# Two NF4 matrices turned within an attention's last batch, and the order of the start: a four-layer kernel on one core

## What is computed

```python
x = x + _L0_xattn_ref(_layernorm(x), ctx, w_in, b_in, w_out, b_out, w_ct, b_ct, 64)
x = x + _L0_ffn_ref(_layernorm(x), weight1, weight2, weight3)
...
def _L0_xattn_ref(mask, encodings, ...):      # 16 batches, 8 heads of 16, 512 tokens
    q, k, v = split(mask^T @ w_in.T + b_in)
    scores = where(|i - j| <= 64, q k^T / 4, min)
    o = softmax(scores) v @ w_out.T + b_out
    return (relu(o^T) * encodings) through w_ct, + b_ct
...
def _L0_ffn_ref(x, weight1, weight2, weight3):
    w1, w2, w3 = nf4_roundtrip(each)          # blocks of 64, scales quantised again
    return (silu(x w1^T) * (x w2^T)) w3^T     # 1408 hidden columns
```

## Time and profile before

| | |
|---|---|
| Runs, median (lowest to highest) | 1455.07 us (1453.42 to 1456.38) |
| Profiled execution, its own time | 1452.38 us |
| Its span on the core | 1450.6 us |
| Mean granted clock of PE | 0.979 |
| Busy: PE, DVE, ACT, POOL | 93%, 67%, 54%, 17% |
| First attention, up to the barrier | 0 to 476 us |
| Turning of weights and first rows | 476 to 492.6 us |

### The profile page before, as it was taken

The page is one execution under the profiler, slowest core; times in us unless marked ns, Lnnn a source line. Parts: engine busy times, 40 slices in busy tenths (PEclk is TensorE's granted clock), DMA queues, the critical chain, the costliest instruction groups (busy, mean ns, idle before and its releaser), DMA issues. The chain is left out here.

```text
span 1450.6 us, 28759 instructions
## 1 busy us (share of the span) xinstructions
PE 1355.9 (93%) x8732; PEld 818.1 (56%) x8732; DVE 977.6 (67%) x3234; ACT 788.2 (54%) x1802; POOL 245.7 (17%) x265
## 2 busy tenths in 40 slices
PE   3688999999999899999989999998788999999998
PEld 1345656565555444444455555555434877777774
DVE  6988999999996545546456788777568655444211
ACT  4877888888878533332367666667420233333231
POOL 3100000000000100000011000013311255555452
PEclk7799999999999999999999999999999999999999
DMA  8634353434430400000020000000413588898885
GB/s 258 172 79 99 81 123 96 117 95 111 108 82 10 146 0 0 0 0 1 0 76 15 16 16 14 14 0 31 151 70 111 165 259 251 246 255 251 243 243 116
DMA packets 63186, 149.52 MB, mean 103 GB/s; under 512 B 10792, under 2 KB 27830, under 8 KB 58892
## 3 DMA queue, kind: packets, MB, share of 16 engines
q1 hardware_dynamic: 49836, 115.70, 26.4%
q0 software_dynamic: 13280, 32.93, 9.9%
HBM read 113.21 MB, written 35.39 MB: 102 GB/s over the span
## 5 line engine op out<-in xcount | busy, mean ns | idle before, releaser
L777 DVE CUSTOM_DVE_ANT_0 masked_scores<-ps_max,band_mask 128x192 bf16<-128x192 f32 (+1 forms) x512 | 176.7, 382 | 17.7 <-PE ps_max L508 12.8
L386 ACT ACTIVATE probs_t<-ps_sc 128x448 f32<-128x448 f32 x256 | 139.1, 544 | 67.8 <-PE ps_sc L528 67.7
L1256 PE MATMUL f_ps<-f_xt,w_t 128*128 (+1 forms) x704 | 160.2, 382 | 2.5 <-ACT w_t L1311 2.5
L380 ACT ACTIVATE nf_above<-nf_scaled,nf_sign_at 128x512 f16<-128x512 bf16 x231 | 161.9, 717 | 0.0
L2804 DVE TENSOR_TENSOR d_inter<-d_silu_g,d_su 128x384 f32<-128x384 f32 x32 | 17.7, 554 | 161.7 <-PE d_su L2488 156.4
L1928 ACT ACTIVATE c_probs<-d_sg,c_negmax 128x128 f32<-128x128 f32 x256 | 90.3, 365 | 58.3 <-DVE c_negmax L2013 57.9
L508 PE MATMUL ps_max<-k_stack,q_stack 96*128 96x192 bf16 (+1 forms) x512 | 95.9, 271 | 26.7 <-DMA k_stack<-dr_parts 12.7
L1256 PEld LDWEIGHTS f_ps<-f_xt,w_t 128*128 128x128 bf16 x704 | 69.3, 98 | 86.7 <-issue 4.9
L2321 POOL DMA_INDIRECT out<-d_h,d_scatter_now x64 | 97.3, 1520 | 107.2 <-DMA out<-d_h,d_scatter_now 90.4
L2672 DVE TENSOR_SCALAR d_onehot<-d_slot_no,d_pos 128x192 bf16<-128x192 bf16 x512 | 101.0, 288 | 0.3 <-PE d_lb L2389 0.3
L508 PEld LDWEIGHTS ps_max<-k_stack,q_stack 96*128 96x128 bf16 x512 | 45.7, 100 | 93.8 <-issue 64.0
(11 more groups left out here) (385 smaller groups left out, 2869.3 us busy)
## 6 DMA issues: line engine op xcount, KB each, us to landing
d_wgu<-in_ex_gu SPq DMA_DIRECT2D x32, 1024.0 KB, 6.9
d_wdown<-in_ex_d SPq DMA_DIRECT2D x32, 512.0 KB, 6.1
dr_parts<-qk_parts SPq DMA_DIRECT2D x32, 384.0 KB, 4.9
q_stack<-dr_parts SPq DMA_DIRECT2D x32, 192.0 KB, 2.8
k_stack<-dr_parts SPq DMA_DIRECT2D x32, 192.0 KB, 3.4
out<-x_sb SPq DMA_DIRECT2D x21, 256.0 KB, 2.1
nf_w<-in_nf_w POOLq DMA_DIRECT2D x3, 1408.0 KB, 9.3
q_stack<-dr_parts SPq DMA_DIRECT2D x32, 128.0 KB, 2.4
```

The source lines that it names most:

```text
L380: act.activation(above[:, g, k, :], lvl[:, g, :], ACT.Sign, bias=cut[:, k - NDV:k - NDV + 1]).then_inc(s_sg, 1)
L386: act.activation(pt[:, c, :], SP[c % 2][:].rearrange("p a w -> p (a w)")[:, a:z], ACT.Exp, scale=D0 ** -0.5).then_inc(s_e, 1)
L777: op = dve.tensor_tensor_reduce(masked[:, c % 2, k, off:off + hi - lo], M[c % 2][:, k, off:off + hi - lo], mask[:, k, off:off + hi - lo], ...
L1256: mm = pe.matmul(bank[:], w12[:, m, kt, ft * P:(ft + 1) * P], xt[:, q, kt, bass.ds(g * N, N)], start=(kt == 0 and q == 0), stop=(kt == KT ...
```

## The change

There are four edits, and a new memory layout that two of them need. In the code of the change the lines are higher by 17 to 49.

1. **ACT's start.** The second batch's parts stand ahead of all twelve row sums instead of behind four of them.
2. **First maxima.** SP writes and reads them, behind both batches' stack loads and ahead of its loop; POOL goes from the first matrix's maxima straight to the wait for the stacks and the two NF4 loads.
3. **Scales in batch 1.** `block_sums` and `block_recip` stand at step 4 instead of 5 of the first half; `block_scales` stands at step 2 instead of 3 of the second half.
4. **Turning.** The twelve banks of matrices 1 and 2 are turned by PE in batch 15 into the two `ps_max` banks (free there) and copied by DVE: bank 0 at step 2 and 1 to 3 at steps 5 to 7 of the first half, 4 to 11 at steps 0 to 7 of the second. The feed-forward phase turns the six of matrix 3, with x after four (`xs` = 4); the matmul of the hidden scale stands after four banks instead of seven.

For 4 the tile `w12_t` exists from the start. Until batch 15 it holds the q and k stacks of even batches and the scratch of the block maxima (`nf_fold`); those of odd batches are a tile of their own (`stacks_odd`), so POOL's memset of ones is two of half the size, one behind the other. Later phases put tiles of theirs into the same room.

```diff
+CH_W = FF * D // P // CH
+def w12_banks():
+    return [[(m * CH_W * CH + f * D + kt * P, m, f) for f in range(ft, min(ft + 2, FT)) for kt in range(KT)]
+            for ft in range(0, FT, 2) for m in range(2)]
...
+    EARLY_AT = [[[], [], [0], [], [], [1], [2], [3]], [[4], [5], [6], [7], [8], [9], [10], [11]]]
+    turned_bank = lambda n: M[n % 2][:].rearrange("p a w -> p (a w)").bitcast(BF16)[:, 0:len(early[n]) * P]
...
             for i in range(2):
                 write_parts(i, i)
                 for g in range(2):
                     load_stack(i, i, g, 16)
+            sp.wait_ge(s_mp, 2)
+            sp.dma_start(dr_max[0].rearrange("c a t -> a c t"), mparts[:]).then_inc(s_mw0, 16)
+            sp.wait_ge(s_mw0, 16)
+            sp.dma_start(qst[0][96:98, 0:4, :], dr_max[0].rearrange("c (h q) t -> c h (q t)", h=4)).then_inc(s_mr0, 16)
...
             pool.wait_ge(s_am, 1)
             gather_maxima(0, 1)
-            pool.wait_ge(s_mp, 2)
-            pool.dma_start(dr_max[0].rearrange("c a t -> a c t"), mparts[:]).then_inc(s_mw0, 16)
-            pool.wait_ge(s_mw0, 16)
-            pool.dma_start(qst[96:98, 0, 0:4, :], dr_max[0].rearrange("c (h q) t -> c h (q t)", h=4)).then_inc(s_mr0, 16)
             pool.wait_ge(s_ld[0], 192)
...
             root(2, DVE_ROWS)
-            for b in range(DVE_ROWS, DVE_ROWS + 4):
-                row_sum(b)
             for k in range(2):
                 first_part(1, 1, k)
             for k in range(2):
                 second_part(1, k)
-            for b in range(DVE_ROWS + 4, NB):
+            for b in range(DVE_ROWS, NB):
                 row_sum(b)
...
+            def turn_w12(n):
+                if n == 0:
+                    pe.wait_ge(s_nw, 2 * CH_W)
+                    pe.wait_ge(s_mx, 8 * 2 * NB)
+                if n == 1:
+                    pe.wait_ge(s_mp, 4 * NB)
+                if n >= 2:
+                    pe.wait_ge(s_wTc, n - 1)
+                bank = turned_bank(n)
+                for t, (col, m, f) in enumerate(early[n]):
+                    mm = pe.transpose(bank[:, t * P:(t + 1) * P], wn[:, col:col + P], identb[:])
+                mm.then_inc(s_wT, 1)
...
+                    if final:
+                        for n in EARLY_AT[0][c]:
+                            turn_w12(n)
...
+            def copy_w12(n):
+                m, f0, cnt = early[n][0][1], early[n][0][2], len(early[n])
+                dve.wait_ge(s_wT, n + 1)
+                dve.tensor_copy(w12[:, m, :, f0 * P:f0 * P + cnt // KT * P].rearrange("p k (f c) -> p f k c", c=P),
+                                turned_bank(n).rearrange("p (f k c) -> p f k c", k=KT, c=P)).then_inc(s_wTc, 1)
...
-                    if c == 5 and second:
+                    if c == 4 and second:
                         block_sums(1, 3)
                         block_recip(1, 3)
...
-                    if c == 3 and second:
+                    if c == 2 and second:
                         block_scales(1, 3)
...
         for ft in range(0, FT, 2):
-            for m in range(2):
-                out.append([(m * 5632 + f * D + kt * P, m, f) for f in range(ft, min(ft + 2, FT)) for kt in range(KT)])
-        for ft in range(0, FT, 2):
             out.append([(2 * 5632 + kt * FF + f * P, 2, f) for f in range(ft, min(ft + 2, FT)) for kt in range(KT)])
...
-    order, on_act, xs, count = [], [], 11, {"a": 0, "d": 0}
+    order, on_act, xs, count = [], [], 4, {"a": 0, "d": 0}
```

81 lines of the change are left out of this document (50 added, 31 removed).

## The result

| | before | changed |
|---|---|---|
| median of the runs shown, us | 1455.07 | 1461.52 |
| profiled execution, us | 1452.38 | 1457.74 |
| its span, us | 1450.6 | 1456.0 |
| mean granted clock of the span | 0.979 | 0.974 |

The ratio of the times is 1.0056, with a 95% interval of 1.0041 to 1.0072: slower by 8 us (6 to 10.5); the two medians of the table lie 6.45 apart, which that interval takes in. By either number the result is outside the range of the prediction, 1451.0 to 1459.0. In a later comparison the changed kernel had 1.0060 (1.0041 to 1.0078). The change makes the kernel slower, by more than 0.2%.

A forecast was written before the change was run, and what follows sets the result against it. The prediction took PE as the bound, nine tenths busy in nearly every slice, with gains only where PE waits. Its terms, 0 + 1.8 - 1.9 + 4.5 - 4.6 + 0.5, gave +0.3: 1455.4 us, range 1451.0 to 1459.0.

The forecast's parts named there:

- The four places: Where the change touches waits: the start, the second batch, the last batch, and the start of the feed-forward phase.
- term 3: Second batch: block scales one step earlier shrink DVE's 2.32 wait and gain 1.9 us, bounds 0 and -2.3.
- term 2: Start: first maxima on SP go behind the stack loads, their read lands late for PE: +1.8 us, 0 to 3.6.
- Term 5: Start of the feed-forward phase: fewer banks and copies bring the hidden products 4.6 us sooner, bounds -4 and -5.2.
- Term 6: TensorE's clock behind the feed-forward head: the 1.2 GHz stretch reaches further into hidden products, +0.5 us, bounds -1.7 and +1.7.
- signs of being wrong: Last batch grows by under 3 us, PE waits over 3 us for first maxima, or the whole start gets shorter.
- Term 1: Start: ACT's second-batch parts, moved ahead of four row sums, still wait for the first batch's write: 0.
- rival (b): Start: the first maxima's read lands beyond 47 under the NF4 loads; net +3.8 us, 1458.9; chance 0.15.
- Term 4: Last batch: turning twelve banks costs PE 88 transposes, nearly none hidden, +4.5 us, bounds 2.5 and 5.1.
- rival (a): Last batch: the turning hides beside the softmax, term 4 is 2.5 or less; about -2.9 us, 1452.2; chance 0.25.
- Rival (c): Feed-forward head: sparse work keeps PE at 1.2 GHz into the hidden products; net +2.0 us, 1457.1; chance 0.1.

The follow-up runs named there:

- fillers: Transposes of the identity that compute nothing, added to keep PE at work in the head: on the turning alone 0.9994, on nine banks 0.9986, on the kernel before 0.9999.
- the turning alone: The kernel before with only the turning of the twelve banks in the last batch, parts 1, 2 and 3 undone: 1.0023 of the kernel before.
- the memset held: The turning alone, all six remaining banks turned ahead of x's rows, POOL's memset held until DVE has written the last row's halves: 1.0009 of the kernel before.
- the two kernels with nine banks: Turning alone, rows last and memset held, but three of twelve banks back in the head: 1.0021; the same with identity transposes keeping PE at work: 0.9986.

## Why the prediction was wrong

**What bounds the kernel, and the places.** The four places were the right ones, and at each the wait named is the one that changed. The sum was +0.3 and the times show +8.1. Two terms make up most of the gap: term 3 forecast a gain of 1.9 that is not there, and term 2 was too small by 1.2 to 3.1. Terms 5 and 6 add a little each. The range was also too narrow for the terms: with every term at its bad bound (0, +3.6, 0, +5.1, -4.0, +1.7) they add up to +6.4, or 1461.5, while the range ended at 1459.0 and was said to take in the bounds of the terms. At the good end terms 2, 3 and 5 give -2.5 and not -3. One of the signs of being wrong that the prediction named came true: a wait of over 3 us for the first maxima, which was 4.32.

**Term 1 (ACT's order, 0): right.** 1.0002 (0.9988 to 1.0016) alone.

**Term 2 (first maxima on SP, +1.8, bounds 0 to 3.6): too small, and the step that failed is "I take 1.8, the middle, since the NF4 loads are only beginning".** Alone it costs +3.0 (1.2 to 4.9), taken out of the changed kernel it gives back 4.9 (1.7 to 8.1). The queue position was read rightly. The write went out at 41.88, not 40.5, of which 1.0 is this execution's later start (SP's twelve stack loads begin at 35.92, before at 34.88) and 0.3 their length (5.91 against 5.60). Its read was issued 3.36 later, as the row of the same arrangement had said. What was off is the transfer: to PE's start it took 5.5, beyond the 5.0 of the busiest small transfer before, because POOL, freed of the maxima, had started 2.8 MB of loads 3.3 ahead of it. The text had this mechanism, down to the loads that start sooner, and made it the upper bound and rival (b); the middle of an interval was no estimate when a sentence of its own said in what order the two transfers would start. The page that let SyncE's path gain 0.8 (the Trainium skill, "DMA: Bandwidth & Descriptors", Specifications) did not decide: the transfer's own 1.5 in quiet against 2.0 on POOL's queue agrees in sign, and is small beside the 4 us that the traffic adds.

**Term 3 (scales a step earlier, -1.9): no gain was there. The step that failed is "This falls ahead of PE's 1.89 wait and is covered".** The 2.32 wait went, and the scales landed earlier. But the maxima's parts were put behind 3.75 us of DVE work, and PE needs them twice: through the DMA, which I costed, and directly, because they are read from the bank that PE's next product for the maxima overwrites (it waits for s_mp ahead of c = 5). That direct wait I did not look for. It is 3.32 in one piece, nothing covers it, and the granted clock behind it is 0.57. The sum had also left out PE's wait of 2.35 behind the same eleven steps before, which is gone as well; so PE waits 4.24 before and 3.32 now, and the clock behind it can take that back: 1.7 of it goes there. Alone the edit costs +1.2 (-0.7 to +3.2): the gain of 1.9 is ruled out, a loss is not shown.

**Term 4 (turning in the last batch, +4.5): right in the main.** +4.30, 88 transposes at 49 ns; the last PV stands 4.3 later when the lag from the start is taken off (472.26 - 4.58 = 467.7, forecast 468). Three banks fewer give 1.33, 55 ns a transpose: next to nothing of it is hidden, so rival (a) is out.

**Term 5 (the head, -4.6): -4.0.** First hidden product 12.3 after the first turning (485.19 to 497.47), forecast 11.8. The 0.5 is what a half clock adds to the last turnings: two rows at 1.0 instead of 0.6 and twelve transposes at 1.48. With PE kept at work in the same order of the head it is gone: the head is 0.46 shorter.

**Term 6 (clock, +0.5): the kind was right and the size is open.** Rival (c) describes what the trace shows: half clock through the last turnings and into the hidden products. The clock lost around the head is 5.12 or 6.84 in each profiled execution with the changed kernel's order of the head, not 1.72; with fillers it is 0. What of that costs time is smaller. In the seven executions traced with that order the first group takes 0.2 to 1.2 more than in the kernel before, beside the 0.5 that stands in term 5, and +0.5 lies within that. By the times it may be more: keeping PE at work takes 4.2 (1.3 to 7.1) off the turning alone, of which up to 1.7 is what the kernel before loses too, so some 2.5 could be the turning's own; the interval is too wide to tell this from the traces. I argued "the clock will fall no later, and the stretch can reach further", and took less than one stretch for it; the head I forecast (four banks, then one short turn for each row) left PE 1.23 of work in a window of 4 us, where the sparsest of the old head had 1.82. This agrees with the Trainium skill ("TensorE: Matmul & The Clock Gate", What's actually happening), whose rule that the throttle is the default and work releases it I gave with this term, and the fillers show it: they compute nothing and the clock stays.

**The sum.** Alone, the parts cost 0.3, 3.0, 1.2 and 3.3, together 7.8; the whole 8.1 to 8.7. They add up, each with an interval of about 2 either way. What is not settled: the stretches of the turning alone add up to +0.7 in its trace, its times to +3.3 (1.2 to 5.4), and no row shows the rest.

## What to carry to other kernels

When an instruction moves to another queue, ask what the old queue does sooner now that it is free; here it was the load that then starved the moved transfer. When a block of work moves ahead on an in-order engine, list everything that was ahead of it and who waits for that directly, through a semaphore on a shared bank as well as through a DMA. And before thinning out a stretch of TensorE's work, look at what follows: a shorter but sparser head left the next products at 1.2 GHz, and 60 transposes that compute nothing took that away, 1.9 us in the trace and 5 (3 to 7) by the times.

## What was new about the hardware

POOL's memset of 128x4096 f32 (3.52 us) and a DVE TENSOR_SCALAR of 128x512 f32 stand in each other's way: 3.35 instead of 0.55, the end 0.28 behind the memset's; two other kernels with the memset held have 0.54 to 0.55 in all four. The form matters: two DVE copies from PSUM that ran inside the held memset took 1.29 together, as long as outside one (0.69 and 0.68 in the turning alone). The Trainium skill ("SBUF — State Buffer", Who interferes with whom) describes an exclusive lock on a port pair that DVE and GpSimd share; the row agrees.

From the issue of a transfer of 8 KB to PE's start it took 1.5 us with two loads of 1.4 MB held back, and 5.5 and 5.75 us with them: in one kernel they had been issued 3.3 before it, in the other 1.0 before it. The DMA share was 1.03 in the first.

In the stretches where PE waits for others (45 to 120 us), the same kernel comes out differently in each execution: the changed kernel was 4.58 behind at batch 13 in one and 7.68 in another. Single traces of such a stretch differ by 3 us and, between the two kernels with nine banks, by 4.5.
